# Cross-attention block on one core: one V product per stack issued a step earlier, and the second activation placed ahead of the last output's parts

## The chip, the core and the metric

The kernel runs on one core of a Trainium2 chip. The metric is device time in microseconds (us) of one execution; the median of three is taken. All matrices are fp32; large projections and the feed-forward part are computed with each operand split into a high and a low half (fp32r), three matmuls for one product.

The engines named below are TensorE (PE in the rows; PEld is its weight load), VectorE (DVE), ScalarE (ACT), GpSimd (POOL) and SyncE (SP, which only issues DMAs here). Each runs its own list of instructions in order and meets the others only at semaphores.

## What is computed

Four batches, 512 query rows, 512 context rows, width 512, 16 heads of 32. Shortened from the reference:

```python
x = layer_norm(hidden, ln1_w, ln1_b)
q = (x @ q_w + q_b)            # (B, 16, 512, 32) by heads
k = (ctx @ k_w + k_b); v = (ctx @ v_w + v_b)
scores = where(mask, q @ k^T / sqrt(32), min)
out = softmax(scores) @ v
hidden = out @ cproj_w + cproj_b + hidden
y = layer_norm(hidden, ln2_w, ln2_b)
y = gelu(y @ fc_w + fc_b) @ proj_w + proj_b
return hidden + y
```

## The kernel before

There are three stages. The projections of V, K and Q come first (up to about 155 us), then attention (to about 403 us), then the feed-forward part (to the end). Attention works on 16 **stacks** of four heads each (four stacks to a batch), and each stack has four **steps**, one for every 128 context rows: `i` counts the 64 steps, `s` is the stack and `kc` (0 to 3) the step in it. In the words below "first step" is kc 0, "second step" kc 1, and so on.

What TensorE does in a step, by the helpers' names:

- `s1(group)` (L579, four matmuls with 32 rows each) gives four tiles of rough scores for the stack two ahead. It is there only for the row maxima: VectorE reduces the four tiles by `maximum` (L1009, an instruction and a short read of its accumulator, `mx`). The four tiles lie in ring B, four PSUM banks, so `s1` of the next step waits (`v_rb`) until all four maxima of this step are out.
- `s2(i, j)` (L594, j = 0 to 3) gives the exact transposed scores of one head less its maxima. ScalarE makes their exponentials (`exp`, L797) into the tiles `Pt`. The score tiles lie in ring A, three banks that are freed by the exponentials.
- `pv(i)` (L610, four products with 32 columns each, shown as x8 in the trace, x4 in the instruction order) is the V product of step i: exponentials of step i times V, added up over the four steps of a stack in bank 7. Four matmuls work on different columns of the array. It waits for the exponentials of its step (`a_ra`), and the one with kc 0 also for the copy of the finished sum of the last stack out of bank 7 (`a_pv`, ScalarE's `copy_pv`, L819).
- `turn_maxima` (L586) in first steps, `sums` (L625, the denominators, 16 rows in the trace) in third steps, and `cproj` (L487 to L489, six matmuls, half of the output projection of one 128-row block of the batch before) in steps named by the table `PIECES`: all odd steps from 17 to 55, and 56 to 59. A `cproj` puts its result into ring B too, and VectorE adds it to the residual (L1144) behind the maxima of the same step. The next `s1` waits for that addition.

In steps 0 to 55 (`i in GROUPS`) the V product of step i-2 stands in step i: in its middle, behind the second `s2`, for kc 0, 1 and 2, and early, behind `s1`, for kc 3. So the product of a stack's last step, 4s-1, stands in the second step of the next stack, and ScalarE copies bank 7 there (`copy_pv(s - 1)` with kc 1, after two exponentials).

VectorE does in a step: four maxima; in third steps `divide_a` (transpose of the sums), in fourth steps `divide_b`, in first steps of stacks 2 to 14 `divide_t` (L1024, a transpose, 0.7 us) behind the maxima; the residual addition L1144 where a `cproj` stands; in some steps parts of the second layer norm (L932, L937, L960).

The feed-forward loop runs over 64 steps (four batches by 16 slabs of `fc_w` and `proj_w`): `fc(i)` is 12 matmuls on TensorE, `gelu(i)` (L832) one activation on ScalarE, then VectorE splits the result into `HR` (L1178 high, L1180 low), and `pj(i)` is 12 matmuls on TensorE, issued behind `fc(i + 1)`. The last stack's output is divided, biased (L803) and split (L809) at the start of this loop: `divide_a` to `divide_c` (L1014, L1018, L1024, L1032) stand on VectorE behind the split of step 0, and `split_out(15)` (L803 and L809) on ScalarE behind `gelu(0)`, and it waits for L1032.

Of the kernel before, what the change touches and what calls it, by code (L numbers as in the profile page):

```python
# [5 lines left out]
def cross_attention_block(nc: bass.Bass, x, ctxT, mask, vecs, q_w, k_w, v_w, c_w, c_b, fc_w, pj_w, pj_b, out):  # L6
# [16 lines left out]
    with ctx:  # L23
# [86 lines left out]
        def bank(i):  # L110
            return ps[i // 2][:, i % 2, :]
# [50 lines left out]
        def evicted(u):  # L162

            b, n = divmod(u, 12)
            if u == 47:
                return "a_qb", 1
            return ("a_v", 4 * b + n + 1) if n < 4 else ("v_ql", 8 * b + n - 3)
# [8 lines left out]
        GROUPS = {i: EARLY + i for i in range(NI) if EARLY + i < 4 * NS}  # L176
# [306 lines left out]
        def _(eng):  # L483
# [27 lines left out]
            def proj_T(b, g, which, hs=(0, 1)):  # L511
                u = 12 * b + (8 if which else 4) + g
                wt = WKQ[2 * which:2 * which + 2]
                acts = XT[b % 2] if which else CT[b % 2]
                for h in hs:
                    if which:
                        pe.wait_ge("v_hi", 5)
                        if h:
                            pe.wait_ge("a_hi", 7)
                        pe.wait_ge("g_lo", 2 + h)  # L520
                        pe.wait_ge("a_xh", 4 * b + 2 + 2 * h)
                        pe.wait_ge("g_xl", 4 * b + 2 + 2 * h)
                    else:
                        pe.wait_ge("a_hi", 5 + h)
                        if h:
                            pe.wait_ge("v_lo", 9)
                        else:
                            pe.wait_ge("g_lo", 1)
                    if h == 0:
                        if u >= 44:  # L530
                            pe.wait_ge(*evicted((41, 42, 44, 45)[u - 44]))
                        else:
                            pe.wait_ge(*evicted(u - 4))
                    for k in (2 * h, 2 * h + 1):
                        ins = mm3(bank(proj_bank(u)), [w[:, k, g * 128:(g + 1) * 128] for w in wt],
                                  [a[:, k, :] for a in acts], k == 0, k == 3)
                if h:
                    ins.then_inc(S["p_pj"], 1)
# [25 lines left out]
            def ring_b(place):  # L564
                if place >= 4:
                    pe.wait_ge("v_rb", place - 3)
                else:

                    pe.wait_ge("v_fu", 13 + place)
                return bank(bank_b(place))  # L570

            def s1(group):

                s, qc = divmod(group, 4)
                pe.wait_ge(f"d_hi{s % 2}", 32 * (s // 2 + 1))
                ring_b(RB[("s1", 4 * group + 3)])
                for j in range(4):
                    r = slice(32 * j, 32 * j + 32)
                    eng.matmul(bank(bank_b(RB[("s1", 4 * group + j)])), lead(s)[r, 0, qc * 128:(qc + 1) * 128], lead(s)[r, 1, :],  # L579
                               start=True, stop=True).then_inc(S["p_rb"], 1)  # L580

            def turn_maxima(q):
                pe.wait_ge("cst", 2)
                pe.wait_ge("v_rb", RB[("s1", 16 * q + 15)] + 1)
                bk = ring_a(("mt", q))
                eng.transpose(bk[0:16, 0:128], mx[:, q % 2, :], ident[:, :]).then_inc(S["p_ra"], 1)  # L586

            def s2(i, j):
                s, kc = divmod(i, 4)
                Q_, K_ = STK[s % 3]  # L590
                pe.wait_ge(f"d_st{s % 3}", stacked(s))
                pe.wait_ge("d_m", 16 * (s + 1))
                bk = ring_a(("s2", i, j))
                eng.matmul(bk, K_[0:98, j, kc * 128:(kc + 1) * 128], Q_[0:98, j, :],  # L594
                           start=True, stop=True).then_inc(S["p_ra"], 1)

            def pv(i):
                s, kc = divmod(i, 4)
                b, g = divmod(s, 4)
                pe.wait_ge("a_ra", RA[("s2", i, 3)] + 1)  # L600
                pe.wait_ge("a_v", 4 * (b + 1))
                if kc == 0:
                    if s:
                        pe.wait_ge("a_pv", s)
                    else:
                        pe.wait_ge(*evicted(47))
                for j in range(4):
                    r = (2 * i + j // 2) % 6
                    c = (4 * g + j) * 32
                    ins = eng.matmul(bank(7)[32 * j:32 * j + 32, :], V[:, 4 * b + kc, c:c + 32], Pt[:, r, j % 2, :],  # L610
                                     start=kc == 0, stop=kc == 3)
                ins.then_inc(S["p_pv"], 1)

            def sums(s):
                pe.wait_ge("cst", 3)
                if s < NS - 1:
                    bk = ring_a(("sm", s))
                else:
                    pe.wait_ge("a_ra", NA)
                    bk = bank(6)  # L620
                for m in (2 * s, 2 * s + 1):
                    pe.wait_ge(*added(2 * m + 1, 0))
                    pe.wait_ge(*added(2 * m + 1, 1))
                    for j in range(4):
                        ins = eng.matmul(bk[32 * j:32 * j + 32, :], ones[:, :], pair(m)[:, j, :], start=m % 2 == 0, stop=m % 2 == 1)  # L625
                ins.then_inc(S["p_sm"], 1)

            def cproj(b, c, ks, outp):
                pe.wait_ge("g_wc", ks[-1] + 1)
                pe.wait_ge("a_ah", 4 * b + ks[-1] + 1)  # L630
                pe.wait_ge("g_al", 4 * b + ks[-1] + 1)
                for k in ks:
                    ins = mm3(outp, [a[:, k, c * 128:(c + 1) * 128] for a in AT], [w[:, k, :] for w in WC], k == ks[0], k == ks[-1])
                return ins
# [61 lines left out]
            for i in range(NI):  # L696
                s, kc = divmod(i, 4)
                b = i // 16
                if i == 2:
                    proj_T(*LAST_Q, 1, (1,))  # L700
                if kc < 3:
                    s2(i, 0)
                if i in GROUPS:
                    s1(GROUPS[i])
                if i >= 2 and (kc == 3 or i not in GROUPS):
                    pv(i - 2)
                if i == 0:
                    proj_T(*LAST_Q, 1, (0,))
                if kc < 3:
                    s2(i, 1)  # L710
                if i in TURNS:
                    turn_maxima(TURNS[i])
                if i >= 2 and kc < 3 and i in GROUPS:
                    pv(i - 2)
                if kc == 2 and s:
                    sums(s - 1)
                if kc == 3:
                    s2(i, 0)
                    s2(i, 1)
                if i in PIECES:  # L720
                    n, c, half = PIECES[i]
                    bk = ring_b(RB[("cp", n, c, half)])
                    cproj(n, c, (2 * half, 2 * half + 1), bk).then_inc(S["p_rb"], 1)
                s2(i, 2)
                s2(i, 3)
# [22 lines left out]
        def _(eng):  # L748
# [72 lines left out]
            def gelu(i):  # L821
                b, f = divmod(i, NF)
                n = i % 2
                g = HN[:, n, :] if i < 12 else R1[:, n, :]
                act.wait_ge("p_fc", i + 1)
                if i < 2:
                    act.wait_ge("g_xl", 20)
                elif i in (12, 13):
                    act.wait_ge(*quotient(NS - 1))
                else:  # L830
                    act.wait_ge("v_hl", i - 1)
                eng.activation(g, bank(4 + i % 2), ACT.Gelu_apprx_tanh, bias=fcb[:, f:f + 1]).then_inc(S["a_g"], 1)  # L832
# [50 lines left out]
            for i in range(NI):  # L883
                s, kc = divmod(i, 4)
# [32 lines left out]
            for i in range(NJ):  # L917
                b, f = divmod(i, NF)
                gelu(i)
                if i == 0:  # L920
                    split_out(NS - 1)
                if b + 1 < B and 13 <= f < 15:
                    for k in (2 * f - 26, 2 * f - 25):
                        y_high(b + 1, k)
# [462 lines left out]
```

## Time and profile before

| | |
|---|---|
| median of three runs | 771.12 us (771.04 to 771.34) |
| the profiled execution, its own time | 771.11 us |
| its span, first to last instruction | 769.3 us |
| TensorE's mean granted clock | 0.999 of full speed |
| busy: TensorE, VectorE | 744.1 us (97%), 457.1 us (59%) |
| busy: GpSimd, ScalarE | 299.1 us (39%), 281.4 us (37%) |
| products L610 | 512 rows, 68.2 us |

The span lies 1.8 us below the profiled execution's time; the rest is start and end of the launch. A row of the timeline has start and duration in us, engine, line, operation, tiles and a count; in brackets stands the idle time ahead of it and what ended it. Starts of successive rows are what counts on TensorE: matmuls overlap in the pipeline, so a row can be longer than the distance to the next.

### The profile page before, as it was taken

To read this page: it belongs to the slowest core of one execution; us is meant where nothing else is said; L and a number is where in the kernel's file an instruction comes from. 1 tells how busy PE (TensorE), PEld (TensorE's weight loads), DVE (VectorE), ACT (ScalarE), POOL (GpSimd) and SP (SyncE) were. 2 spreads that over 40 slices of the span, in tenths; PEclk is the share of its full clock that TensorE was granted. 3 is DMA by queue.
4 is the path that set the end of the run, shared out by engine and by line. 5 is a ranking of instruction groups with operands and counts; after the bars stand their busy time and mean duration, and the time that the engine had idled before them with its cause. 6 is when DMAs were issued, how large, how long until landed. Compare 5 with 4: busy or idle time off the path is not lost.

```text
span 769.3 us, 10036 instructions
## 1 busy us (share of the span) xinstructions
PE 744.1 (97%) x3664; PEld 514.2 (67%) x3664; DVE 457.1 (59%) x995; ACT 281.4 (37%) x492; POOL 299.1 (39%) x183
## 2 busy tenths in 40 slices
PE   7999999989999999999999999999999999999998
PEld 5878886733344444444436888888888888888886
DVE  6673347778888888898697668443424333232213
ACT  4534241276766566667682011211112111211110
POOL 2654150068998778798754002212002200220000
PEclk9999999999999999999999999999999999999999
DMA  9656377597666785678641537240220413030001
GB/s 328 231 167 214 136 220 240 193 268 167 158 164 146 184 216 145 156 209 177 176 136 53 181 109 202 74 165 0 42 69 18 147 18 93 1 109 1 1 0 55
DMA packets 94385, 103.25 MB, mean 134 GB/s; under 512 B 39968, under 2 KB 48420, under 8 KB 94336
## 3 DMA queue, kind: packets, MB, share of 16 engines
q1 hardware_dynamic: 94192, 102.59, 46.5%
q8 instruction: 29, 0.48, 0.2%
q14 instruction: 20, 0.16, 0.1%
q10 hardware_dynamic: 144, 0.02, 0.0%
HBM read 73.08 MB, written 29.37 MB: 133 GB/s over the span
## 4 chain that ended last, share of the span: by engine, by line
PE 80%; DVE 12%; issue 3%; ACT 2%; DMA 1%; POOL 1%; SPq 0%; ACTq 0%; DVEq 0%
PE ps L487 22%; PE ps L488 21%; PE ps L489 21%; DVE ps L1009 6%; PE ps L594 4%; PE ps L610 4%; PE ps L579 4%; PE ps L625 3%; DVE R L1144 2%; ACT Pt L797 1%; PE ps L547 1%; DVE mx L1009 1%; DMA qs<-BIG 1%; DVE R L945 1%; DVE st L932 1%
## 5 line engine op out<-in xcount | busy, mean ns | idle before, releaser
L797 ACT ACTIVATE Pt<-ps 128x512 f32<-128x512 f32 x256 | 137.6, 598 | 70.9 <-PE ps L594 69.6
L1178 DVE CAST HR<-R 128x512 fp32r<-128x512 f32 x52 | 24.9, 478 | 186.0 <-ACT R L832 186.0
L832 ACT ACTIVATE R<-ps,cols 128x512 f32<-128x512 f32 x52 | 35.9, 690 | 227.2 <-PE ps L489 227.1
L594 PE MATMUL ps<-BIG 98*128 98x512 f32 x256 | 93.2, 439 | 3.6 <-ACT Pt L797 3.2
L1009 DVE CUSTOM_DVE_ANT_0 ps<-ps,FU 128x512 f32<-128x512 f32 x128 | 84.6, 724 | 14.9 <-PE ps L579 14.8
L1009 DVE CUSTOM_DVE_ANT_0 ps<-ps,BIG 128x512 f32<-128x512 f32 x128 | 84.6, 723 | 10.8 <-PE ps L579 10.7
L594 PEld LDWEIGHTS ps<-BIG 98*128 98x128 f32 x256 | 44.2, 187 | 68.3 <-issue 29.3
L487 PE MATMUL ps<-BIG,HR 128*128 128x512 f32 x192 | 74.8, 390 | 1.0 <-DVE HR L1180 1.0
L487 PE MATMUL ps<-YT,BIG 128*128 128x512 f32 x192 | 74.9, 390 | 0.0
L488 PE MATMUL ps<-YT,BIG 128*128 128x512 f32 x192 | 74.7, 389 | 0.0
L489 PE MATMUL ps<-BIG,HR 128*128 128x512 f32 x192 | 74.7, 389 | 0.0
L489 PE MATMUL ps<-YT,BIG 128*128 128x512 f32 x192 | 74.7, 389 | 0.0
L488 PE MATMUL ps<-BIG,HR 128*128 128x512 f32 x192 | 74.7, 389 | 0.0
L610 PE MATMUL ps<-Pt,V 128*32 128x512 f32 x512 | 68.2, 605 | 0.0
L1325 POOL TENSOR_TENSOR R<-Pt 128x1024 f32<-128x1024 f32 x20 | 47.3, 2388 | 45.9 <-ACT Pt L797 45.9
L1221 POOL TENSOR_TENSOR BIG<-R,BIG 128x512 fp32r<-128x512 f32 (+1 forms) x31 | 42.2, 1388 | 42.1 <-ACT BIG L809 22.8
L487 PE MATMUL ps<-BIG 128*128 128x512 f32 x128 | 52.8, 413 | 5.8 <-DVE BIG L1077 5.8
L1221 POOL TENSOR_TENSOR YT<-R,YT 128x512 fp32r<-128x512 f32 x12 | 15.5, 1308 | 109.1 <-ACT YT L849 109.1
L1325 POOL TENSOR_TENSOR RAWY<-Pt 128x1024 f32<-128x1024 f32 x22 | 52.0, 2385 | 4.8 <-ACT Pt L797 4.8
L488 PE MATMUL ps<-BIG 128*128 128x512 f32 x128 | 50.9, 398 | 0.0
L487 PE MATMUL ps<-BIG,WK 128*128 128x512 f32 x128 | 50.8, 397 | 0.0
L489 PE MATMUL ps<-BIG 128*128 128x512 f32 x128 | 50.7, 396 | 0.0
(132 smaller groups left out, 1371.3 us busy)
## 6 DMA issues: line engine op xcount, KB each, us to landing
BIG<-qs SPq DMA_DIRECT2D x62, 256.0 KB, 2.8
BIG<-ks SPq DMA_DIRECT2D x62, 256.0 KB, 3.2
ks<-BIG SPq DMA_DIRECT2D x32, 256.0 KB, 2.0
qs<-BIG SPq DMA_DIRECT2D x32, 256.0 KB, 5.8
R<-hd SPq DMA_DIRECT2D x28, 256.0 KB, 3.9
R<-in_x SPq DMA_DIRECT2D x16, 256.0 KB, 5.4
hd<-R SPq DMA_DIRECT2D x16, 256.0 KB, 3.2
yt<-FU SPq DMA_DIRECT2D x64, 64.0 KB, 1.9
```

The lines of the kernel that those rows point to most:

```text
L487: eng.matmul(outp, a[0], b[0], start=first, stop=False)
L488: eng.matmul(outp, a[1], b[0], start=False, stop=False)
L489: return eng.matmul(outp, a[0], b[1], start=False, stop=last)
L579: eng.matmul(bank(bank_b(RB[("s1", 4 * group + j)])), lead(s)[r, 0, qc * 128:(qc + 1) * 128], lead(s)[r, 1, :], start=True, stop=True).the ...
L594: eng.matmul(bk, K_[0:98, j, kc * 128:(kc + 1) * 128], Q_[0:98, j, :], start=True, stop=True).then_inc(S["p_ra"], 1)
L610: ins = eng.matmul(bank(7)[32 * j:32 * j + 32, :], V[:, 4 * b + kc, c:c + 32], Pt[:, r, j % 2, :], start=kc == 0, stop=kc == 3)
L797: eng.activation(Pt[:, r, j % 2, :], bank(bank_a(("s2", i, j))), ACT.Exp, scale=SCALE).then_inc(S["a_ra"], 1)
L832: eng.activation(g, bank(4 + i % 2), ACT.Gelu_apprx_tanh, bias=fcb[:, f:f + 1]).then_inc(S["a_g"], 1)
L1009: eng.tensor_tensor_reduce(out=scores, in0=scores, in1=MASK[s // 4], scale=1.0, scalar=-3.4e38, op0=ALU.add, op1=ALU.max, accum_out=mx[:, ...
L1178: eng.tensor_copy(HR[:, n, 0, :], g).then_inc(S["v_hh"], 1)
L1221: eng.tensor_tensor(dst, src, high.bitcast(F32), ALU.subtract).then_inc(S[name], 1)
L1325: eng.tensor_tensor(pair(m)[:, 2 * hp:2 * hp + 2, :], Pt[:, (r - 2) % 6, :, :], Pt[:, r, :, :], ALU.add).then_inc(S["g_ac"], 1)
```

## The change

Two places are touched. In attention, a first step (kc 0) now issues two V products in its middle, those of i-2 and i-1, a second step (kc 1) none, a third step (kc 2) that of i-2 as before; fourth steps and steps from 56 on are as they were. So in 13 stacks (1 to 13) the product of the last step of the stack before moves from the second step to the first, right behind the product that stands there. On ScalarE, `split_out(15)` moves from behind `gelu(0)` to behind `gelu(1)`. No work is added or removed, and no semaphore changes.

```diff
-                if i >= 2 and kc < 3 and i in GROUPS:
-                    pv(i - 2)
+                if i in GROUPS:
+
+                    if kc in (0, 2) and i >= 2:
+                        pv(i - 2)
+                    if kc == 0 and i:
+                        pv(i - 1)
...
             for i in range(NJ):
                 b, f = divmod(i, NF)
                 gelu(i)
-                if i == 0:
+                if i == 1:
                     split_out(NS - 1)
```

On TensorE, before, in stack 5, from the maxima's transpose of its first step (L586) to the `cproj` of its second step (L487):

```order
L586 MATMUL ps<-ident,mx 16x128 [waits s_a_ra]
L610 MATMUL ps<-Pt,V 32x512 x4
L594 MATMUL ps<-BIG 128x512 [waits s_a_ra] x3
L579 MATMUL ps<-BIG 128x512 [waits s_v_rb]
L579 MATMUL ps<-BIG 128x512 x3
L594 MATMUL ps<-BIG 128x512 [waits s_a_ra]
L610 MATMUL ps<-Pt,V 32x512 x4
L487 MATMUL ps<-BIG 128x512 [waits s_v_rb]
```

The same stretch with the change:

```order
L586 MATMUL ps<-ident,mx 16x128 [waits s_a_ra]
L610 MATMUL ps<-Pt,V 32x512 x8
L594 MATMUL ps<-BIG 128x512 [waits s_a_ra] x3
L579 MATMUL ps<-BIG 128x512 [waits s_v_rb]
L579 MATMUL ps<-BIG 128x512 x3
L594 MATMUL ps<-BIG 128x512 [waits s_a_ra]
L487 MATMUL ps<-BIG 128x512 [waits s_v_rb]
```

The second product went from behind the second step's `s1` (L579) to ahead of it; the number of waits is the same. In stacks 1 to 3 there is no `cproj`, and three more L594 follow where L487 stands here.

On ScalarE, at the head of the feed-forward loop, before (L819 is the last copy of bank 7, L832 the activations, L803 and L809 the two parts of the last output):

```order
L819 ACTIVATE BF<-ps 128x512 [waits s_p_pv]
L832 ACT_TABLE_LOAD [waits s_g_xl]
L832 ACTIVATE HN<-ps,cols 128x512 [waits s_p_fc]
L803 ACTIVATE R<-R,cols 128x512 [waits s_v_at]
L809 ACTIVATE BIG<-R 128x512 [waits s_a_ab]
L832 ACTIVATE HN<-ps,cols 128x512 [waits s_p_fc]
```

and with the change (the lines of the changed file are four further down):

```order
L823 ACTIVATE BF<-ps 128x512 [waits s_p_pv]
L836 ACT_TABLE_LOAD [waits s_g_xl]
L836 ACTIVATE HN<-ps,cols 128x512 [waits s_p_fc] x2
L807 ACTIVATE R<-R,cols 128x512 [waits s_v_at]
L813 ACTIVATE BIG<-R 128x512 [waits s_a_ab]
```

The second activation no longer stands behind the instruction that waits for VectorE's quotient (`v_at`).

## Rows read from the trace of the kernel before

**Rows 1.** Page, part 1: busy time, share of the span, instructions
```profile
PE 744.1 (97%) x3664; PEld 514.2 (67%) x3664; DVE 457.1 (59%) x995; ACT 281.4 (37%) x492; POOL 299.1 (39%) x183
```

**Rows 2.** Windows: length, busy PE, PEld, DVE, ACT, POOL, clock, DMA share, GB/s
```profile
404.00:769.00 365.00, 360.97 (x1598) 296.90 (x1596) 154.19 (x272) 53.56 (x79) 49.04 (x37) 1.00 0.24 70
```

**Rows 3.** TensorE's waits, by releaser: us in total, times, longest
```profile
PE ps L579 <- DVE mx L1009: 7.4, 19, 0.8
PE ps L579 <- DVE R L1144: 2.9, 13, 0.3
PE ps L487 <- DVE HR L1180: 1.0, 1, 1.0
```

**Rows 4.** Timeline of TensorE, stack 2: `s1` of its second and third step
```profile
182.66 0.51 PE L579 MATMUL ps<-BIG 32*128 32x512 f32 x4 [0.37 <-DVE mx L1009]
...
185.96 0.51 PE L579 MATMUL ps<-BIG 32*128 32x512 f32 x4 [0.48 <-DVE mx L1009]
```

**Rows 5.** Timeline of TensorE, stack 6: first, second and start of third step
```profile
241.99 1.06 PE L610 MATMUL ps<-Pt,V 128*32 128x512 f32 x8
242.98 0.96 PE L594 MATMUL ps<-BIG 98*128 98x512 f32 x3
244.28 0.51 PE L579 MATMUL ps<-BIG 32*128 32x512 f32 x4 [0.33 <-DVE mx L1009]
244.71 0.50 PE L594 MATMUL ps<-BIG 98*128 98x512 f32 x1
245.15 1.07 PE L610 MATMUL ps<-Pt,V 128*32 128x512 f32 x8
246.14 0.50 PE L487 MATMUL ps<-BIG 128*128 128x512 f32 x1
...
248.60 0.50 PE L579 MATMUL ps<-BIG 32*128 32x512 f32 x4
```

**Rows 6.** Timeline of VectorE, stack 6, second step: first maximum and residual addition
```profile
244.80 0.70 DVE L1009 CUSTOM_DVE_ANT_0 ps<-ps,BIG 128x512 f32<-128x512 f32 x1
...
247.85 0.69 DVE L1144 TENSOR_TENSOR R<-ps,R 128x512 f32<-128x512 f32 x1 [0.34 <-PE ps L489]
```

**Rows 7.** Timeline of VectorE, stack 9, second step, behind its fourth maximum
```profile
296.02 0.69 DVE L932 BATCH_NORM_STATS2 st<-HN 128x6 f32<-128x512 f32 x1
296.63 0.68 DVE L1144 TENSOR_TENSOR R<-ps,R 128x512 f32<-128x512 f32 x1
```

**Rows 8.** Timeline of TensorE: sixteen and eight matmuls of the sums
```profile
250.34 1.90 PE L625 MATMUL ps<-RAWY,ones 128*32 128x512 f32 x16
...
380.95 1.04 PE L625 MATMUL ps<-R,ones 128*32 128x512 f32 x8
```

**Rows 9.** Timeline of ScalarE, start of the feed-forward part
```profile
412.74 0.72 ACT L803 ACTIVATE R<-R,cols 128x512 f32<-128x512 f32 x1 [5.80 <-DVE R L1032]
...
414.03 0.68 ACT L832 ACTIVATE HN<-ps,cols 128x512 f32<-128x512 f32 x1
```

**Rows 10.** Timeline of VectorE, same stretch: the splits of activations 0 and 1
```profile
409.17 0.41 DVE L1178 CAST HR<-HN 128x512 fp32r<-128x512 f32 x1
409.62 0.69 DVE L1180 TENSOR_TENSOR HR<-HN,HR 128x512 fp32r<-128x512 f32 x1
...
414.74 1.05 DVE L1178 CAST HR<-HN 128x512 fp32r<-128x512 f32 x1 [2.04 <-ACT HN L832]
415.82 1.65 DVE L1180 TENSOR_TENSOR HR<-HN,HR 128x512 fp32r<-128x512 f32 x1
```

**Rows 11.** Timeline of GpSimd, same stretch
```profile
414.20 1.30 POOL L1221 TENSOR_TENSOR BIG<-R,BIG 128x512 fp32r<-128x512 f32 x1 [6.10 <-ACT BIG L809]
415.45 3.15 POOL L1254 TENSOR_TENSOR R<-R,cbt 128x512 f32<-128x512 f32 x2
```

**Rows 12.** Timeline of TensorE, same stretch: starts of pj(0) and pj(1)
```profile
410.89 0.39 PE L487 MATMUL ps<-BIG,HR 128*128 128x512 f32 x1
...
417.52 0.50 PE L487 MATMUL ps<-BIG,HR 128*128 128x512 f32 x1 [1.03 <-DVE HR L1180]
```

## The prediction, made before the changed kernel was run

> **What bounds the kernel now.** First the busy times: TensorE is busy 97% of the span [rows 1], and from 404 us on 360.97 of 365 us at full clock [rows 2]. So a microsecond gained or lost ahead of the feed-forward part reaches the end whole, and there is no later slack that gives it back. TensorE's waits are few [rows 3]. The largest is `s1` behind VectorE's maxima, 7.4 us in 19 waits; then `s1` behind the residual addition L1144, 2.9 us in 13; and one wait of 1.0 us on `HR`. The first kind sits in attention, and there the timeline of both engines has to be read step by step.
>
> A second step begins when its `s1` starts, and that start waits for VectorE in every changed stack: 0.37 us in stack 2 [rows 4], 0.33 us in stack 6 [rows 5]; over the 13 stacks it is 0.31 to 0.37 us, nearly the same each time. The third step's start has three forms:
> - Stacks 1 to 3, without a `cproj`: again VectorE decides (wait 0.48 us in stack 2), and the second step takes 185.96 - 182.66 = 3.30 us [rows 4]. That is the loop `s1`, four maxima, next `s1`.
> - Stacks 4 to 8 and 11 (six): TensorE decides. In stack 6 VectorE stands idle for 0.34 us until the `cproj` is ready, then adds, and the third step's `s1` starts at once [rows 5, 6]. The second step takes 248.60 - 244.28 = 4.32 us [rows 5].
> - Stacks 9, 10, 12 and 13 (four): VectorE has a piece of the second layer norm more, as L932 in stack 9, and L1144 follows without any idle time [rows 7]. VectorE decides here too.
>
> **The change in the first step.** One V product more. Its price is eight more rows of the same kind behind eight: the sums show sixteen at 1.90 us and eight at 1.04 us [rows 8], so 0.86 us. The upper bound is a product followed by other work, 242.98 - 241.99 = 0.99 us [rows 5]; the two share a tiling of the array, so I take 0.86. What it reads has long been there: the exponentials of the step before are out before the first of the two products ends, so no wait is added. The next `s1` had a wait of about 0.34 us, and this is all that covers the product: 0.86 - 0.34 = 0.52 us remain, and `s1` of the second step starts that much later, in all 13 stacks. VectorE's first maximum started 244.80 - 244.28 = 0.52 us behind it [rows 5, 6], and keeps that distance; the transpose that VectorE does in between ended just before that start, so it gives no room for the delay either.
>
> **The change in the second step.** One product less, which frees TensorE for 246.14 - 245.15 = 0.99 us [rows 5]. Whether that returns depends on who decides:
> - Stacks 1 to 3: VectorE's loop of 3.30 us stays as it is, nothing returns. 3 x 0.52 = +1.6 us. In stack 1 ScalarE's exponentials are a little late in the third step anyway, which may hide 0.1 us: I take +1.5.
> - Six stacks: VectorE's chain was 0.34 us short of deciding [rows 6]. Its own shift is 0.52 us, so L1144 starts 0.52 - 0.34 = 0.18 us later than now. The `cproj` can't start as early as TensorE is free, for it takes the bank of the first maximum, which ends at about 244.80 + 0.52 + 0.75; so it starts near where it starts now and ends ahead of the fourth maximum. 6 x 0.18 = +1.1 us.
> - Four stacks: VectorE decides already, so the whole shift passes. 4 x 0.52 = +2.1 us.
>
> Third and fourth steps keep their order and their lengths. ScalarE's copy of bank 7 no longer waits for the product, but who waits for that copy is the product of the third step, long behind. Of moved queues there are no others: the product issues no DMA, and ScalarE, VectorE, GpSimd and SyncE keep their order in attention. Sum for attention: 1.5 + 1.1 + 2.1 = **+4.7 us**.
>
> One sentence of the Trainium skill speaks for the change: "TensorEngine Tiling (Array Packing)", Key Properties, says that changing the tiling mode drains TensorE. The rows show 0.99 us from a product to other work against 0.86 us for one more product of the same kind [rows 5, 8], so a change of mode saved is worth 0.13 us here. By the rule and nothing else 13 stacks would gain 1.7 us; by the rows that time is TensorE's, which doesn't decide.
>
> **The change at the head of the feed-forward part.** ScalarE sits 5.80 us ahead of L803, waiting for VectorE's quotient, and `gelu(1)` stands behind it, at 414.03 us [rows 9]. Its input, `fc(1)`, is done when `pj(0)` starts, at 410.89 us, give or take 0.2 us for the pipeline [rows 12]. Then `pj(1)` waits 1.03 us for `HR` [rows 12]. With the change `gelu(1)` runs at about 411.1 to 411.8 us. VectorE is busy with the quotient until 412.7 us (L803 starts at 412.74 [rows 9]) and then splits at once: 0.41 + 0.69 us as for activation 0 [rows 10], done by 413.9 us. `pj(1)` can follow `fc(2)` directly, at 417.52 - 1.03 - 0.1 = 416.4 us. The wait goes whole, and with it the refill behind it (a row of 0.50 us in place of 0.39 us): **-1.2 us**. L803 and L809 start when they do now, so nothing behind them is later. What is next late there would be the split of slab 3 on VectorE, which moves ahead by about 3 us and has its time until after `pj(1)`.
>
> The same place shows a contention. The split of activation 1 takes 1.05 + 1.65 us where that of activation 0 takes 0.41 + 0.69 [rows 10]; GpSimd is running then [rows 11]. The Trainium skill, "SBUF — State Buffer", the section on the two separate sides, says that VectorE and GpSimd hold a shared port pair exclusively for an instruction. By the rows alone: if the split in its new place took 2.70 us it would end at 415.4 us, and still 1 us ahead of 416.4.
>
> **Sum.** The profiled execution took 771.11 us, its span 769.3 us, the median of the runs is 771.12 us. 771.11 + 4.7 - 1.2 = **774.6 us**, slower by 0.45%.
>
> **The rivals.**
> 1. *TensorE decides in the second step* (the other side). The place is the second step's `s1` and the third's. If the maxima let `s1` go earlier than the rows suggest, the wait of 0.34 us is filled by the product and the 0.99 us returns whole: 0.86 - 0.34 - 0.99 = -0.47 us a stack, 13 stacks -6.1 us, and with the head of the feed-forward part 763.8 us. It decides where VectorE's chain from `s1` to `s1` is under 3.3 us without a `cproj` and under 3.8 us with one. Against it: the chain is 3.30 us without one [rows 4], and with one 0.52 + 4 x 0.65 + 0.75 = 3.9 us (the fourth maximum and L1144 follow one another at 0.65 us). Chance 0.05.
> 2. *It returns in the six stacks only.* If L1144 there can start as soon as TensorE is ready, as it does now, these give 6 x -0.47 = -2.8 us instead of +1.1, and attention as a whole +0.8 us: 770.7 us. For it: that is where TensorE decides now. Against it: four maxima stand ahead of L1144 on VectorE. Chance 0.07.
> 3. *The gain at the head doesn't come.* VectorE could be held elsewhere (the split of slab 3 now starts while GpSimd works), and `pj(1)` or `pj(2)` waits as long as before: 771.11 + 4.7 = 775.8 us. Against it are the 2.5 us between 413.9 and 416.4. Chance 0.08.
> 4. *ScalarE becomes the bound of stacks 1 to 3.* The two `s2` behind the products come 0.86 us later there, and ring A has three banks, so the second step's `s2` wait for exponentials. The slack by the rows is some 0.5 us; if it is used up, or if the added product costs 0.99 us, 13 x 0.13 = 1.7 us come on top: 776.3 us. Chance 0.10.
> 5. *A part of the shift is hidden* at places that I count as passing it on (a stack whose fourth step waits for ScalarE, the end of attention, where TensorE waits for exponentials): about half the +4.7 gone, 772.3 us. Chance 0.10.
>
> **How the numbers follow.** The forecast gets 0.60; its own range is 773.6 to 775.6 us. Two runs of this kernel can be told apart from about 0.2%, here 1.5 us, that is outside 769.6 to 772.7. Faster: rival 1, and some of 2, 0.07. Same: most of 2, and part of 5, 0.11. Slower: the rest, 0.82. The range of 8 in 10 takes in the forecast, rivals 3 and 4 and a part of 5: 772.6 to 776.4 us.
>
> **What would show each step.** Right: `s1` of second steps starts without a wait, and first steps take about 3.8 us instead of 3.3; second steps of stacks 1 to 3 still take 3.3 us; in second steps with a `cproj` its first matmul waits for a maximum, and L1144 follows the maxima with no idle time; the waits of L579 for the maxima fall from 7.4 to about 3 us; ScalarE's `gelu(1)` starts near 3 us earlier against `fc(1)`, and the wait of 1.03 us is gone. Wrong: second steps with a `cproj` of 3.4 us, or first steps under 3.5 us, would mean that VectorE is not what decides; a wait of `pj(1)` or `pj(2)` for `HR` would take the second gain back.

## The result

The changed kernel takes 775.47 us (median of four runs, 775.28 to 777.66), the kernel before 771.08 us (770.75 to 771.34): ratio 1.0064, 95% interval 1.0045 to 1.0082 (the ratio is taken over all runs, so it isn't quite that of the medians). That is slower by 4.4 us by the medians; the forecast was 3.5 us slower. The profiled execution has a span of 773.6 us against 769.3 us, and a mean granted clock of 0.996 against 0.999.

TensorE's waits in the changed kernel (releaser, us in total, times, longest), to be held against [rows 3]; lines behind the first hunk have moved by four, so L1013 is the maxima and L1148 the residual addition:

```profile
PE ps L579 <- DVE R L1148: 5.2, 14, 0.8
PE ps L594 <- ACT Pt L801: 4.8, 11, 0.7
PE ps L487 <- DVE mx L1013: 4.1, 10, 0.4
PE ps L579 <- DVE mx L1013: 3.5, 7, 0.8
```

Of the second of these the kernel before had:

```profile
PE ps L594 <- ACT Pt L797: 3.2, 8, 0.7
```

The wait of `s1` for the maxima fell from 7.4 us to 3.5. That for the residual addition rose from 2.9 to 5.2, that of `s2` for ScalarE's exponentials from 3.2 to 4.8. There is a new one, `cproj` (L487) for a maximum, ten times about 0.4 us, and the one of `pj(1)` for `HR` is gone. Waits explain only a part, though. The starts of `s1` give the length of each step. Apart from stack 1's third step, 4.36 us before and 4.24 after, no step differs by more than 0.04 us except these (us, read off the L579 rows of both traces):

| step | before | after | times | sum |
|---|---|---|---|---|
| first, stacks 1 to 13 | 3.25 to 3.29 | 3.72 to 3.73 | 13 | +5.9 |
| second, stacks 1 to 3 | 3.29 to 3.33 | 3.28 | 3 | -0.1 |
| second, stacks 4 to 8 and 11 | 4.29 to 4.32 | 3.82 to 3.84 | 6 | -2.8 |
| second, stacks 9, 10, 12, 13 | 4.43 to 4.49 | 4.42 to 4.50 | 4 | 0 |
| third, stacks 2 and 3 | 4.25, 4.24 | 5.88, 5.95 | 2 | +3.3 |

The sum is +6.3; the other steps took 0.2 us less and the projections were done 0.4 us earlier in this execution, so the last `s1` starts 5.7 us later, at 373.03 us instead of 367.36, and `pj(1)` 4.5 us later. The first four lines were forecast in kind. The last was not.

Stack 6 in the changed kernel, TensorE from its first step on, to be held against [rows 5]:

```profile
245.94 1.92 PE L610 MATMUL ps<-Pt,V 128*32 128x512 f32 x16
247.79 0.96 PE L594 MATMUL ps<-BIG 98*128 98x512 f32 x3
248.69 0.51 PE L579 MATMUL ps<-BIG 32*128 32x512 f32 x4
249.12 0.49 PE L594 MATMUL ps<-BIG 98*128 98x512 f32 x1
250.03 0.50 PE L487 MATMUL ps<-BIG 128*128 128x512 f32 x1 [0.42 <-DVE mx L1013]
...
252.52 0.50 PE L579 MATMUL ps<-BIG 32*128 32x512 f32 x4
```

and VectorE in its second step, to be held against [rows 6]:

```profile
249.22 0.70 DVE L1013 CUSTOM_DVE_ANT_0 ps<-ps,BIG 128x512 f32<-128x512 f32 x1 [0.48 <-PE ps L579]
249.84 0.73 DVE L1013 CUSTOM_DVE_ANT_0 ps<-ps,BIG 128x512 f32<-128x512 f32 x1
...
251.14 0.73 DVE L1013 CUSTOM_DVE_ANT_0 ps<-ps,BIG 128x512 f32<-128x512 f32 x1
251.78 0.68 DVE L1148 TENSOR_TENSOR R<-ps,R 128x512 f32<-128x512 f32 x1
```

The two products take 247.79 - 245.94 = 1.85 us, up to the next matmul's start, against 0.99 for one, so 0.86 us for the second, as forecast. `s1` of the second step no longer waits. L1148 follows the fourth maximum without idle time.

What happened in stack 2 is best seen in windows that are its second and third step, first of the kernel before, then of the changed one (length, busy time of TensorE, its weight loads, VectorE, ScalarE, GpSimd, each with its number of instructions, then the granted clock, the DMA share and GB/s):

```profile
182.66:185.96 3.30, 2.82 (x17) 1.02 (x18) 3.22 (x9) 3.09 (x7) 3.30 (x3) 1.00 0.93 258
185.96:190.21 4.25, 4.25 (x32) 1.35 (x32) 3.23 (x9) 1.49 (x4) 4.25 (x3) 1.00 1.07 224
```

```profile
182.95:186.23 3.28, 2.27 (x9) 0.93 (x8) 2.79 (x9) 3.28 (x8) 3.28 (x4) 1.00 0.86 264
186.23:192.11 5.88, 5.88 (x31) 1.57 (x31) 3.21 (x9) 1.62 (x4) 5.62 (x3) 0.71 1.08 232
```

The second step had 2.82 us of TensorE work and now has 2.27. In the third step, whose order did not change, the clock was granted at 0.71 of full in the mean. In windows of 1 us it stands at 0.50 or 0.51 (1.2 GHz instead of 2.4) from 187 to 190 us:

```profile
186.00:187.00 1.00, 0.77 (x5) 0.38 (x5) 0.41 (x3) 1.00 (x3) 1.00 (x1) 1.00 1.04 242
187.00:188.00 1.00, 1.00 (x9) 0.22 (x12) 1.00 (x3) 0.72 (x2) 1.00 (x1) 0.51 1.04 240
188.00:189.00 1.00, 1.00 (x12) 0.34 (x8) 1.00 (x5) 0.00 (x0) 1.00 (x2) 0.50 1.08 248
189.00:190.00 1.00, 1.00 (x12) 0.22 (x8) 0.47 (x2) 0.00 (x0) 1.00 (x1) 0.50 1.08 215
```

The eight rows of a product take 1.93 us there (L610; L625 are the sums):

```profile
187.12 1.93 PE L610 MATMUL ps<-Pt,V 128*32 128x512 f32 x8
188.83 1.83 PE L625 MATMUL ps<-RAWY,ones 128*32 128x512 f32 x8
```

Eight rows of the sums take 1.83 us. In the same step of the kernel before these rows took 1.06 and 1.04 us. The same happens in stack 3 from about 204 to 208 us. So the open question was whether the change causes the clock's fall, and by what.

The head of the feed-forward part in the changed kernel, ScalarE, VectorE and TensorE, against [rows 9, 10, 12]:

```profile
416.75 0.69 ACT L836 ACTIVATE HN<-ps,cols 128x512 f32<-128x512 f32 x1 [4.15 <-PE ps L489]
418.41 0.72 ACT L807 ACTIVATE R<-R,cols 128x512 f32<-128x512 f32 x1 [0.96 <-DVE R L1036]
```

```profile
418.29 0.42 DVE L1182 CAST HR<-HN 128x512 fp32r<-128x512 f32 x1
418.74 0.69 DVE L1184 TENSOR_TENSOR HR<-HN,HR 128x512 fp32r<-128x512 f32 x1
...
420.02 3.49 DVE L1048 TENSOR_TENSOR BIG<-RW,BIG 128x512 fp32r<-128x512 f32 x2
423.43 1.52 DVE L1182 CAST HR<-HN 128x512 fp32r<-128x512 f32 x1
```

```profile
421.99 0.39 PE L487 MATMUL ps<-BIG,HR 128*128 128x512 f32 x1
```

`gelu(1)` runs as soon as its input is there, its split takes 0.42 + 0.69 us where it took 1.05 + 1.65, and `pj(1)` starts without a wait, 2.6 us after the split is done. The slowing next to GpSimd didn't vanish: it now meets the split of slab 3 (3.49 us for two instructions that took 1.28 before) and of activation 2 (1.52 us), while GpSimd runs from 419.87 to 424.67 us. Nobody waits for these.

### The profile page after: what moved, and what is told of

Same layout as the page of the kernel before. It is cut to its first block, busy times and chain, and to the rows that moved or that the text cites. A ratio compares the mean times of both kernels' runs of the same rounds, so it can differ in the third digit from the quotient of the medians.

```text
span 773.6 us, 10036 instructions
## 1 busy us (share of the span) xinstructions
PE 745.5 (96%) x3664; PEld 515.8 (67%) x3664; DVE 454.6 (59%) x995; ACT 279.5 (36%) x492; POOL 299.0 (39%) x183
## 4 chain that ended last, share of the span: by engine, by line
PE 86%; DVE 10%; ACT 2%; issue 2%; DMA 0%; POOL 0%; SPq 0%; DVEq 0%; ACTq 0%
PE ps L487 21%; PE ps L488 21%; PE ps L489 21%; PE ps L610 7%; PE ps L594 6%; DVE ps L1013 5%; PE ps L625 4%; PE ps L579 4%; DVE R L1148 2%; ACT Pt L801 1%; PE ps L547 1%; DVE R L949 1%; DVE mx L1013 1%; DVE st L936 1%; DMA RAWY<-in_ctxT 0%
## 5 line engine op out<-in xcount | busy, mean ns | idle before, releaser
L594 PE MATMUL ps<-BIG 98*128 98x512 f32 x256 | 93.8, 441 | 5.2 <-ACT Pt L801 4.8
L1013 DVE CUSTOM_DVE_ANT_0 ps<-ps,FU 128x512 f32<-128x512 f32 x128 | 84.6, 722 | 17.0 <-PE ps L579 17.0
L1013 DVE CUSTOM_DVE_ANT_0 ps<-ps,BIG 128x512 f32<-128x512 f32 x128 | 84.6, 722 | 14.4 <-PE ps L579 14.4
L594 PEld LDWEIGHTS ps<-BIG 98*128 98x128 f32 x256 | 44.3, 187 | 69.0 <-issue 38.2
L487 PE MATMUL ps<-YT,BIG 128*128 128x512 f32 x192 | 74.9, 390 | 0.0
L487 PE MATMUL ps<-BIG,HR 128*128 128x512 f32 x192 | 74.7, 389 | 0.0
L610 PE MATMUL ps<-Pt,V 128*32 128x512 f32 x512 | 66.9, 614 | 0.0
L487 PE MATMUL ps<-BIG 128*128 128x512 f32 x128 | 52.5, 410 | 9.9 <-DVE BIG L1081 5.8
L487 PE MATMUL ps<-BIG,WK 128*128 128x512 f32 x128 | 50.9, 398 | 0.3 <-POOL BIG L1225 0.3
```

The lines of the kernel that those rows point to most:

```text
L487: eng.matmul(outp, a[0], b[0], start=first, stop=False)
L1013: eng.tensor_tensor_reduce(out=scores, in0=scores, in1=MASK[s // 4], scale=1.0, scalar=-3.4e38, op0=ALU.add, op1=ALU.max, accum_out=mx[:, ...
```

## The experiments

Each is compared with the kernel before on the same chip. The four sets of experiments were on four different chips, so a difference between kernels of two sets is less sure than one within a set. "Second half" below is the move of `split_out(15)`, "first half" that of the products.

### Each half alone

The diff of the first kernel is the last hunk of the change alone, that of the second the first hunk alone.

> Only the second half of the change: split_out(15) behind gelu(1), all V products where they were. My theory: pj(1)'s wait of 1.03 us for HR goes with its refill, 1.2 us, and the attention part is that of before: 771.1 - 1.2 = 769.9 us. Rival (another instruction on VectorE becomes late in its place): no gain, 771.1 us.

Measured: 769.22 us (768.87 to 770.29, 11 runs) against 770.87; ratio 0.9979, interval 0.9970 to 0.9988. The mean clock was 1.000 in every run, and the wait for `HR` is gone.

> Only the first half of the change: the 13 products moved, split_out(15) behind gelu(0) as before. If the two halves add up: 775.5 + 1.2 = 776.7 us, with the clock low for some 3.5 us in the third steps of stacks 2 and 3 again. If the clock's fall has to do with something else than the products, it is absent here and the time is 776.7 - 3.3 = 773.4 us.

Measured: 777.34 us (775.61 to 779.48, five runs); ratio 1.0083, interval 1.0068 to 1.0098. The clock is low in the third steps of stacks 2 and 3 again, 5.94 us each, and `pj(1)` waits 1.1 us for `HR`. The halves add up within what the runs scatter: the second is worth 1.65 us alone and 1.9 us on top of the first (across two sets of runs), the first costs 6.5 us. The clock's fall belongs to the products.

### Which stacks lower the clock

```diff
-                if i in GROUPS:
-
-                    if kc in (0, 2) and i >= 2:
+                if i in GROUPS and i >= 2 and kc < 3:
+                    if kc != 1 or not (s >= 4):
                         pv(i - 2)
-                    if kc == 0 and i:
+                    if kc == 0 and (s >= 4):
                         pv(i - 1)
```

So the products of stacks 1 to 3 stay in their second steps.

> The whole change, but stacks 1 to 3 keep their product in the second step; 10 of the 13 products are moved. Theory A (the clock falls because a second step without a product and without a cproj leaves TensorE little to do): no second step of that kind is left, the clock stays full, attention is 10 x 0.45 - 6 x 0.47 = +1.7 us, with the head of the feed-forward part -1.2 us: 771.6 us. Theory B (two products in a row make the clock fall): it falls somewhere in stacks 4 to 13 too, 3 us more: 774 us or over.

Measured: 771.50 us (770.57 to 773.61, 11 runs); ratio 1.0011, interval 1.0002 to 1.0020. The profiled execution has its third steps of stacks 2 and 3 at 4.25 and 4.25 us. The expectation of the first theory was 771.6. The mean clock was 0.999 or 1.000 in ten of the runs; one had 0.997 and took 773.61 us. Ten pairs of products in a row don't lower the clock by themselves. A single run of that kind occurs without any moved product too: of the 74 runs of the kernel before in all these sets, four had a mean clock of 0.997 and took 772.94 to 774.15 us. None of them was profiled, so where the clock fell in them isn't known.

The other way round, only stacks 1 to 3 changed (`0 < s < 4`):

> The whole change, but only stacks 1 to 3 get their product in the first step. If all of the loss beyond the steps' own lengths is the clock in these three stacks: 3 x 0.43 = +1.3 us, +3.3 us for the clock, on 769.2 us of the second half alone: 773.8 us, with the clock low in third steps of stacks 1 to 3 and nowhere else. If the clock's fall needs the later stacks' order as well, 770.5 us.

Measured: 773.74 us (772.48 to 775.44, seven runs); ratio 1.0036, interval 1.0022 to 1.0051. In the profiled execution, the fastest but with a mean clock of 0.998, only one third step was slow, stack 2's (5.94 us); in the other six the mean clock was 0.993 to 0.996. One fall in a profile goes with a mean clock of 0.998, two with 0.995 or 0.996, so by this measure (an estimate for the runs without a profile) most of the others had two: how many of the three stacks are hit differs from run to run.

### Work put into the empty steps

In the second steps of stacks 1 to 3 each matmul of `s2` is issued twice:

```diff
                 bk = ring_a(("s2", i, j))
+                if kc == 1 and 0 < s < 4:
+                    eng.matmul(bk, K_[0:98, j, kc * 128:(kc + 1) * 128], Q_[0:98, j, :], start=True, stop=True)
                 eng.matmul(bk, K_[0:98, j, kc * 128:(kc + 1) * 128], Q_[0:98, j, :],
```

> The whole change, and in the second steps of stacks 1 to 3 every score matmul L594 is issued twice into the same bank (the first of the two is overwritten): four extra matmuls a step at about 0.23 us, 0.9 us of work in a step where TensorE waits about 1 us. Theory A (too little TensorE work in these steps lets the clock fall): the clock stays full, second steps stay near 3.3 us, third steps of stacks 2 and 3 are back at 4.25 us instead of 5.9: 775.5 - 3.4 = 772.1 us. Theory B (the two products in a row, or something else in the order): the clock falls as before, 775.5 us or more by the added work.

Measured: 772.91 us (772.66 to 773.61, ten runs), ratio 1.0026, interval 1.0016 to 1.0035, with a mean clock of 1.000 in all ten runs. Stack 2's second and third step as windows:

```profile
183.93:187.22 3.29, 2.55 (x13) 1.35 (x12) 2.70 (x8) 3.29 (x8) 3.29 (x4) 1.00 0.93 275
187.22:191.46 4.24, 4.24 (x32) 1.35 (x33) 3.23 (x9) 1.39 (x4) 4.24 (x3) 1.00 1.06 236
```

Added work makes this kernel 2.6 us faster than the changed one (775.47 us in its own set; by the ratios, 1.0064 and 1.0026, 2.9 us). The third step is back at 4.24 us. The time is 0.8 us above the expected 772.1, most of it because the first of the doubled matmuls stands ahead of the second step's `s1` and lengthens the first step to 3.94 or 3.95 us, three times 0.22. The two products in a row are still there, so they are not the cause; the little work of the second step is. In the changed kernel 2.27 and 2.25 us busy of 3.28 went ahead of the two falls, and here, with 2.55 of 3.29, there was none. It isn't the length of a single wait either. The longest in this second step is longer than any in the changed kernel's (0.50 and 0.51 us in stack 2):

```profile
187.22 0.51 PE L579 MATMUL ps<-BIG 32*128 32x512 f32 x4 [0.74 <-DVE mx L1015]
```

In the changed kernel stack 1's third step stayed at 4.24 us after 2.26 busy of 3.28. Over all five profiles with the product taken out of the second steps of stacks 1 to 3 and nothing put in, 9 of the 15 third steps behind were slow. So a second step with so little work makes a fall possible and doesn't settle it; what decides in a given stack stays open.

### What the six stacks give back

The products moved in stacks 4 to 8 and 11 only, together with the second half:

> The whole change, but only stacks 4 to 8 and 11 (those where TensorE decided before when the third step starts) get their product in the first step. The traces so far give 0.46 us more in the first step and 0.47 us less in the second: attention +0 us, with the head of the feed-forward part as in the run with that half alone, 769.2 us. By the prediction's own sum it would be 6 x 0.18 more: 770.3 us.

Measured: 769.70 us (768.73 to 770.06, 11 runs); ratio 0.9981, interval 0.9972 to 0.9990. In stack 4, for one, first and second step are 3.72 and 3.84 us, together 7.56, where they were 3.29 and 4.30; in the six stacks together the sum is that of the kernel before within 0.1 us. Nothing is won or lost there, and the prediction's 0.18 us a stack is refuted.

To see what bounds the second step, one maximum was cut to 32 of 512 columns in the ten second steps with a `cproj`. The other 480 columns are left out of these row maxima. (`m` is written for 0 in the first kernel and for 3 in the second; `s` is here the stack whose maxima are taken, two ahead.)

```diff
-                eng.tensor_tensor_reduce(out=scores, in0=scores, in1=MASK[s // 4], scale=1.0, ...
+                w = 32 if s >= 6 and qc == 1 and j == m else 512
+                eng.tensor_tensor_reduce(out=scores[:, 0:w], in0=scores[:, 0:w], in1=MASK[s // 4][:, 0:w], scale=1.0, ...
```

> The whole change, and in the second steps of stacks 4 to 13 VectorE's first maximum runs over 32 of 512 columns (these row maxima are left out in part). Two chains lead to the third step's start: VectorE's queue (four maxima, L1148), and the bank of the first maximum (first maximum, cproj, L1148). Both lose about 0.45 us here: second steps of stacks 4 to 8 and 11 fall from 3.83 to about 3.4 us, those of 9, 10, 12, 13 from 4.43 to 4.0, all in all 4 us less than the changed kernel. If TensorE's own work decides, they stay at 3.83.

> As the run before, but the fourth maximum is cut instead of the first. If VectorE's queue alone decides, the second steps of stacks 4 to 8 and 11 fall by 0.45 us as there. If the bank of the first maximum binds the cproj just as tightly (in the changed kernel the cproj starts 0.4 us late behind that maximum and ends just ahead of L1148), they fall by 0.05 us at most, and only those of stacks 9, 10, 12, 13, where VectorE has a norm piece in between, fall by about 0.45 us.

Measured, one run each: 773.0 and 775.81 us. The total is disturbed by the clock (0.993 in both; here the third steps of stacks 1 and 3 were slow, stack 1's over 7 us), so the expected 4 us less in the total can't be judged, and the steps are what counts. `s1` of stack 6's second and third step and what lies between, the first maximum cut:

```profile
250.00 0.51 PE L579 MATMUL ps<-BIG 32*128 32x512 f32 x4
250.84 0.50 PE L487 MATMUL ps<-BIG 128*128 128x512 f32 x1
...
253.33 0.51 PE L579 MATMUL ps<-BIG 32*128 32x512 f32 x4
```

and the fourth:

```profile
251.04 0.51 PE L579 MATMUL ps<-BIG 32*128 32x512 f32 x4
252.39 0.50 PE L487 MATMUL ps<-BIG 128*128 128x512 f32 x1 [0.40 <-DVE mx L1014]
...
254.82 0.50 PE L579 MATMUL ps<-BIG 32*128 32x512 f32 x4
```

with L1149, the residual addition of this kernel, on VectorE:

```profile
254.08 0.69 DVE L1149 TENSOR_TENSOR R<-ps,R 128x512 f32<-128x512 f32 x1 [0.30 <-PE ps L489]
```

With the first cut the step takes 3.33 us instead of 3.83, with the fourth 3.78. In stacks 9, 10, 12 and 13, 3.91 to 4.01 us instead of 4.42 to 4.50, in both. For the steps both expectations were met: two chains end together in the six stacks, VectorE's four maxima with L1148, and the first maximum's bank with the `cproj` and L1148. Shortening the last maximum only shows the second chain.

### A product in two halves

If moving the whole product gives nothing because the first step loses what the second wins, moving half of it should win: the wait of 0.33 us in the first step hides most of a half.

```diff
+                if i in GROUPS and i >= 2 and kc < 3:
+                    halved = s in (4, 5, 6, 7, 8, 11)
+                    pv(i - 2, (2, 3) if kc == 1 and halved else (0, 1, 2, 3))
+                    if kc == 0 and halved:
+                        pv(i - 1, (0, 1))
```

The numbers are column groups, one head each. The lines taken out are not shown, nor those in `pv`, which now signals only with group 3.

> The second half of the change, and in stacks 4 to 8 and 11 half of the product (two of its four column groups) in the first step, the other half in the second, where it was. If the wait of 0.33 us for the maxima covers what it covers and no more, four matmuls' 0.43 us there leave about +0.03 us, and the second step falls from 4.30 to 3.87 us, still above the 3.83 us that the other engines' chain needs: 6 x -0.40 = -2.4 us against the run with the head alone: 766.8 us, the fastest so far. If a product cut in two costs a change of tiling more than it saves, or the wait is no cover: 769.2 us or over.

Measured: 771.82 us (771.27 to 772.89, 11 runs); ratio 1.0010, interval 1.0002 to 1.0019. The expectation failed by 5 us. TensorE in stack 6 says why:

```profile
243.19 1.91 PE L610 MATMUL ps<-Pt,V 128*32 128x512 f32 x12
...
246.80 1.05 PE L610 MATMUL ps<-Pt,V 128*32 128x512 f32 x4
247.78 0.50 PE L487 MATMUL ps<-BIG 128*128 128x512 f32 x1
```

Twelve rows take as long as sixteen (1.92 us), four as long as eight. The halved product was paid twice, in the first step (3.72 us) and in the second (4.30). So the cut was made through the 512 query columns instead, 256 of all four heads in each step:

```diff
+                    halved = s in (4, 5, 6, 7, 8, 11)
+                    pv(i - 2, slice(256, 512) if kc == 1 and halved else slice(0, 512))
+                    if kc == 0 and halved:
+                        pv(i - 1, slice(0, 256))
```

The lines taken out are not shown, nor those in `pv`, where only the second half ends the accumulation in bank 7 and signals.

> The second half of the change, and in stacks 4 to 8 and 11 the product cut through the 512 query columns: 256 columns of all four heads in the first step, the other 256 in the second. The product halved by column groups cost as much as a whole one (12 rows took 1.91 us, 16 rows 1.92 us): if that is because the four groups stream side by side, half the columns are half the time, 0.43 us. Then first steps are near 3.3 us, second steps near 3.87 us, 6 x -0.4 us against the second half of the change alone: about 766.9 us. If a product has a price of its own per start, whatever its length, it stays at 769 us or over.

> The second half of the change alone once more, beside the run above on the same chip, as its base. If the two runs' difference is real, it shows here again: 769.2 us against 766.9.

Measured: 767.72 us (767.05 to 769.35, five runs), ratio 0.9964, interval 0.9951 to 0.9978; and its base beside it 770.06 us (769.00 to 771.66, 11 runs), ratio 0.9989, interval 0.9980 to 0.9997. Stack 6:

```profile
240.72 1.50 PE L610 MATMUL ps<-Pt,V 128*32 128x512 f32 x16
242.15 0.97 PE L594 MATMUL ps<-BIG 98*128 98x512 f32 x3
243.04 0.51 PE L579 MATMUL ps<-BIG 32*128 32x512 f32 x4
...
243.91 0.64 PE L610 MATMUL ps<-Pt,V 128*32 128x256 f32 x8
244.48 0.50 PE L487 MATMUL ps<-BIG 128*128 128x512 f32 x1
```

First steps of the six stacks take 3.29 to 3.31 us, second steps 3.86 to 3.94. Both times are 0.8 us above those expected, and their difference of 2.3 us is the expected one; the two intervals don't overlap. This kernel beats both: by the medians it is 3.2 us under the kernel before of its own set, and 7.7 under the changed one, which was measured in another set.

## Why the prediction came out as it did

- *A second V product costs 0.86 us, and the wait of about 0.34 us is all that covers it*: right in kind, a little high in size. It gave 0.52 us; first steps grew by 0.43 to 0.48. A step that begins without a wait runs from the three `s2` to the next `s1` in 0.90 us (247.79 to 248.69); with the wait of 0.33 it took 1.30 [rows 5], so 0.07 us more than the wait went with it. 13 x 0.07 = 0.9 us too much loss.
- *Stacks 1 to 3 give nothing back*: right, their second steps take 3.28 us. *Stacks 9, 10, 12 and 13 neither*: right, 4.42 to 4.50 us as before.
- *The six stacks lose 0.18 us each*: wrong in size, they lose nothing. The term was 0.52 - 0.34. The first number was 0.06 too large, as above. The 0.34 us of idle time [rows 6] counts from the end of the short read behind the fourth maximum, as the rows between the two of [rows 6] show:

```profile
246.72 0.73 DVE L1009 CUSTOM_DVE_ANT_0 ps<-ps,BIG 128x512 f32<-128x512 f32 x1
247.37 0.14 DVE L1009 DVE_READ_ACCUMULATOR2_ANT mx<- 128x1 f32 x1
247.85 0.69 DVE L1144 TENSOR_TENSOR R<-ps,R 128x512 f32<-128x512 f32 x1 [0.34 <-PE ps L489]
```

When the addition can go it starts before that read is done: in the changed kernel 251.78 - 251.14 = 0.64 us behind the fourth maximum's start, where it was 247.85 - 246.72 = 1.13. The slack was about 0.48 us, and the shift of 0.46 uses it up and leaves nothing, as measured. That the `cproj` would wait for the first maximum was right.
- *The head of the feed-forward part gains 1.2 us*: right. The lag behind the kernel before is 5.7 us at the last `s1` and 4.5 us at `pj(1)`. Alone it gave 1.65 us in one set of runs and 0.9 in the other. Rival 3, that this gain doesn't come, fell with it.
- *Third and fourth steps keep their order and their lengths*: this is the step that failed. They kept their order, but the third steps of stacks 2 and 3 took 5.88 and 5.95 us instead of 4.25 and 4.24, at a granted clock of 0.71. That TensorE stays at full clock was taken for granted, and the loss of 3.3 us has no term in the sum. The sum of the other terms as measured is 5.9 - 2.8 - 0.1 - 1.2 = +1.8 us where the prediction had +3.5. So the total came near by luck: two errors of opposite sign, 1.7 us too much loss in the steps and 3.3 us of loss at the clock that were left out. (1.8 + 3.3 is 0.7 us above the measured 4.4; the earlier end of the projections and the other steps account for 0.6 of it.)
- The rivals: the one of a gain in all 13 stacks fell with the stacks 1 to 3. The one of a gain in the six alone fell with the run on them: its -0.47 us a stack needs second steps of 4.32 - 0.99 = 3.33 us, which came only with the first maximum cut short. ScalarE was not the bound of stacks 1 to 3: `s2` waits for it there, but the third step's `s1` still waits 0.51 us for a maximum in stack 2. Nor did a later step hide a part of the shift: stack 1's third step took 4.24 us instead of 4.36, but with the second half of the change alone, no product moved, it took 4.25 too.
- The tiling rule of the Trainium skill ("TensorEngine Tiling (Array Packing)", Key Properties) agrees with the rows: a product costs 0.99 us ahead of other work and 0.86 us behind another product, and for half the columns it is 0.57 and 1.43 - 0.99 = 0.44 us, 0.13 us less both times. That time was again not the one that decides. The port rule of the Trainium skill ("SBUF — State Buffer", the section on the two separate sides) agrees with the slowed work on VectorE, which moved along with GpSimd's: 3.49 us for two instructions next to it, 1.28 without.
- The clock: the Trainium skill, "TensorE: Matmul & The Clock Gate", describes in its section on HAM oscillation a clock gate that takes TensorE down to half its rate within a running kernel, behind stretches without matmuls. The rows agree as to the levels (1.00 and 0.50). That section speaks of long waits for data; the Trainium skill's next section on the same page, on a second failure mode, speaks of short idle times between groups of matmuls that come often. Here stack 2's step ahead of the fall has only short waits (the two longest 0.50 and 0.51 us), and more work in that step kept the clock up. The prediction did not weigh this, and it should have: it speaks against taking a product out of a step that waits for others.

## What to carry to other kernels

Before a product is moved out of a step, look at how much TensorE work remains in that step, not only at who ends it: here 0.55 us less work in a step that didn't get shorter cost 1.6 to 1.7 us in the next one, twice in an execution, and issuing matmuls twice there, for nothing but the work, won most of it back. To move a part of the work into a wait, cut it so that the part is shorter in time (the streamed columns), and make it no larger than the wait.

When idle time in front of an instruction is used as slack, take starts to starts from a place where the same pair runs back to back; the idle time alone was 0.14 us short here, and a wait had 0.07 us of restart behind it.

## What the runs showed of the hardware that was not expected

- TensorE's clock went to half for about 3.5 us right behind steps in which it was busy 2.25 to 2.27 of 3.28 us with no wait over 0.53 us, and for over 6 us in stack 1 of the two kernels with a cut maximum. It stayed full behind 2.55 of 3.29 us, behind 2.82 of 3.30, and also behind 6 of 15 steps with as little work as the first.
- Matmuls on different column groups of the array stream side by side: rows of two groups take as long as rows of four (1.05 and 1.07 us), while half the columns take 0.57 us up to the next matmul's start in place of 0.99.
